# Six graph heads to a turn and to a value product, label sums and key counts in one set of products, first transfers in a fixed order

## What is computed

```python
# layer 0 (shift, scale and gates come from silu(cond) @ w_ada)
k, q, v = split(modulate(ln(x)) @ w_qkv)
x = x + gate_msa * (softmax(q k / 8) v @ w_proj + b_proj)
x = x + gate_mlp * (gelu(modulate(ln(x)) @ w_mlp1 + b_mlp1) @ w_mlp2 + b_mlp2)
# layer 1
self_feat = concat(x, q) @ W_self.T + b_self
for d in range(2):
    A = (adj if d == 0 else swapaxes(adj, 1, 2))[:, :, :20, :]
    aff = where(A.sum(-1) > 0, qh kh / sqrt(8), -9e15) + A @ w_bias + b_bias
    out += softmax(aff) @ self_feat[:, :20] @ Wout[d] + bout[d]     # per head
return x + relu(self_feat + out)
```

## Time and profile before

| | us |
|---|---|
| median of 3 runs (lowest, highest) | 95.21 (93.9, 97.48) |
| the profiled execution: its time | 95.97 |
| its span, first to last instruction | 94.2 |
| around the span | 1.77 |
| busy: PE, DVE, ACT, POOL | 82.9, 69.2, 58.0, 55.7 |

### The profile page before, as it was taken

How to read it: one execution, slowest core, us unless ns; L and a number is a source line. 1 busy time by engine, 2 the same in 40 slices (tenths; PEclk the granted TensorE clock), 3 DMA queues, 4 the chain that set the end, 5 groups by cost and what they waited for, 6 DMA issues and landing times.

```text
span 94.2 us, 4503 instructions
## 1 busy us (share of the span) xinstructions
PE 82.9 (88%) x1936; PEld 64.6 (69%) x1936; DVE 69.2 (73%) x201; ACT 58.0 (62%) x118; POOL 55.7 (59%) x80
## 2 busy tenths in 40 slices
PE   5979999897879999999999977999999989695930
PEld 5968867474657667879767865888777775485810
DVE  3789999898888623577397794598934986779881
ACT  2928629256766559399835888799962496251710
POOL 6769998998952322614463465698407508916640
PEclk9999999999999999999999999999999999999999
DMA  1867754587702370000110000002100021003134
GB/s 36 214 203 241 248 121 156 123 274 206 266 6 55 104 140 7 0 0 7 39 39 7 0 0 10 0 0 46 39 7 0 7 62 27 7 0 74 33 94 114
DMA packets 5971, 7.09 MB, mean 75 GB/s; under 512 B 1024, under 2 KB 4768, under 8 KB 5952
## 3 DMA queue, kind: packets, MB, share of 16 engines
q1 hardware_dynamic: 5664, 6.68, 25.8%
q10 hardware_dynamic: 288, 0.13, 0.5%
HBM read 4.94 MB, written 0.54 MB: 58 GB/s over the span
## 4 chain that ended last, share of the span: by engine, by line
PE 54%; DVE 16%; issue 12%; SPq 6%; DMA 5%; POOL 4%; POOLq 1%
PE ps_all L1063 7%; PE ps_all L1142 6%; PE ps_all L1155 6%; PE ps_all L1106 5%; DMA Vz<-v_raw 5%; PE ps_all L986 4%; SPq L874 4%; PE ps_all L1174 4%; PE ps_all L1069 4%; PE ps_all L1091 3%; PE ps_all L1002 3%; PE ps_all L1096 3%; PE ps_all L1077 2%; PE ps_all L1093 2%; SPq L847 2%
## 5 line engine op out<-in xcount | busy, mean ns | idle before, releaser
L1290 ACT ACTIVATE PT<-ps_all 128x512 f32<-128x512 f32 x24 | 14.1, 596 | 12.9 <-PE ps_all L1155 12.8
L1155 PE MATMUL ps_all<-ident,E 128*128 128x128 f32 x96 | 14.5, 278 | 1.0 <-DVE E L730 1.0
L1155 PEld LDWEIGHTS ps_all<-ident,E 128*128 128x128 f32 x96 | 10.8, 140 | 3.1 <-issue 1.5
L1470 DVE TENSOR_TENSOR E<-ps_all,bias_dir 128x320 f32<-128x320 f32 x16 | 7.8, 489 | 5.2 <-PE ps_all L1142 3.7
L720 POOL TENSOR_TENSOR xT<-gated,xT 128x256 f32<-128x256 f32 x8 | 5.8, 728 | 9.4 <-issue 7.8
L952 POOL TENSOR_TENSOR rstd<-var_eps,minus_half 128x2 f32<-128x2 f32 (+1 forms) x9 | 6.0, 667 | 6.6 <-DVE var_eps L1318 6.3
L1063 PE MATMUL ps_all<-xm,w_rest_sb 128*128 128x256 f32 x32 | 9.7, 390 | 0.0
L730 POOL TENSOR_TENSOR E<-E,neg_max 128x320 f32<-128x320 f32 x8 | 6.2, 774 | 5.4 <-DVE neg_max L1480 5.4
L1223 ACT ACTIVATE hidden<-ps_all,cols 128x256 f32<-128x256 f32 x16 | 7.1, 477 | 3.5 <-PE ps_all L1063 3.4
L1174 PE MATMUL ps_all<-Vz,PT 128*32 128x36 f32 x512 | 7.2, 200 | 1.2 <-issue 1.2
L1174 PEld LDWEIGHTS ps_all<-Vz,PT 128*32 128x32 f32 x512 | 5.9, 109 | 2.7 <-issue 1.4
(11 more groups left out here) (112 smaller groups left out, 201.7 us busy)
## 6 DMA issues: line engine op xcount, KB each, us to landing
home_a<-in_adj SPq DMA_DIRECT2D x2, 448.0 KB, 5.0
Vz<-v_raw SPq DMA_DIRECT2D x16, 45.0 KB
w_rest_sb<-in_w_rest SPq DMA_DIRECT2D x1, 576.0 KB, 5.2
xT<-in_xT SPq DMA_DIRECT2D x1, 512.0 KB
home_a<-in_adj SPq DMA_DIRECT2D x1, 512.0 KB, 4.0
w_rest_sb<-in_w_rest SPq DMA_DIRECT2D x1, 512.0 KB, 5.7
q_tok<-q_rows SPq DMA_DIRECT2D x4, 128.0 KB, 3.5
Vz<-v_raw SPq DMA_DIRECT2D x12, 36.0 KB, 3.1
```

The lines of the kernel that those rows point to most:

```text
L1155: ins = pe.transpose(ps[:, j * P:(j + 1) * P], E[:, r, j * HI:(j + 1) * HI, :], ident[:, :])
L1290: ins = act.activation(PT[:, key % RING, :, :], ps[:, :].rearrange("p (j t) -> p j t", t=P), ACT.Exp)
L1470: ins = dve.tensor_tensor(e_of(key).rearrange("p (j i) k -> p j i k", j=HJ), ps_scores(key), bias_dir[:, d, g, 0:M].unsqueeze(1).unsqueeze ...
```

## The change

- **Turns and values of layer 1.** The arguments of a unit stand as 16 heads of 20 keys without gaps (320 columns and 40 of padding). A turn is three transposes of 120 columns (six heads each), `exp` works on 120 x 384 in place of 128 x 512, and a `values` stage is 3 x 4 products of 54, 54 and 36 columns in place of 4 x 4 of 36.
- **V's places.** `Vz1` has three slots of its own (no part of `Vz0` is reused), each cleared by POOL (2592 columns); mid 3 takes slot 0 again after mid 0's units. A mid's spread is eight DMAs (four of 20 rows with three blocks, four of 20 rows with one) in place of four.
- **Bias.** The adjacency is cut at 121, 121 and 110 rows, 11 whole keys each. One `sel` has label weights in columns 0 to 10 and ones in columns 16 to 26, so that one set of 3 x 4 products without accumulation gives sums and counts. A new DVE stage `btake` (two of them) transposes the results to SBUF; `pen` and `bdir` then read SBUF.
- **Order.** `ORDER` and `BANKS` are new throughout. ACT issues x's group 0 alone; SP issues the others in the order cols, x1, ada0, qkv, x2, x3, x4, ada1. Of the GELU and exp stages, which need different function tables on ACT, all of layer 0's exp now stand ahead of the first GELU and all GELU ahead of layer 1's first exp.

```diff
-ADJ_ROWS = [(0, 112), (112, 224), (224, 352)]
+SIX = 6
+CH = 3
+KR = SIX * M
+EW = CH * KR
+VSLOTS = 3
+KPC = 11
+ADJ_ROWS = [(0, 121), (121, 242), (242, 352)]
...
+BIAS_PARTS = [(0, 1), (2,)]
...
- ('fetch', 'x1'): 'act',
+ ('fetch', 'x1'): 'sp',
...
-        Vz1 = sb("Vz1", [P, HI, (B - VZ0_MIDS_END) * DIRS, HJ, CW])
+        Vz1 = sb("Vz1", [P, VSLOTS, SIX, CH, UB12, DIRS, CW])
...
-        E1 = sb("E1", [P, RING, H, S])
+        E1 = sb("E1", [P, RING, EW])
...
         def vz1_free(m):
-            if batches("v1", m)[2].stop <= VZ0_MIDS_END:
-                return [("values", n) for n in L0_UNITS]
-            return [("zero", ("vz1", m))]
+            if v_before(m) is None:
+                return [("zero", ("vz1", m))]
+            return [("values", n) for n in units_of_mid(v_before(m))]
...
-                    for i in range(HI):
-                        q = slice(QUAD * i, QUAD * i + M)
-                        sp.dma_start(Vz[q, i, :, :, :], v1_raw[q, bs, :, :, :].rearrange("p b d j w -> p (b d) j w"))\
-                          .then_inc(spread_done[key], 16)
+                    nb, k = bs.stop - bs.start, vslot_of(m)
+                    for i in range(SIX):
+                        to = slice(M * i, M * i + M)
+                        for c in range(1 if i < HI else 2):
+                            quad, j, c1 = (i, 0, CH) if i < HI else ((i - HI) * 2 + c, CH, c + 1)
+                            of = slice(QUAD * quad, QUAD * quad + M)
+                            sp.dma_start(Vz1[to, k, i, c:c1, 0:nb, :, :].rearrange("p c b d w -> p c (b d w)"),
+                                         v1_raw[of, j:j + c1 - c, bs, :, :].rearrange("p c b d w -> p c (b d w)"))\
+                              .then_inc(spread_done[key], 16)
...
-                            ins = pe.matmul(ps[QUAD * b:QUAD * b + QUAD, which * G * S:(which + 1) * G * S],
-                                            sel[0:n, which, c, :], t, start=(c == 0), stop=(c == 2))
+                            ins = pe.matmul(ps[QUAD * b:QUAD * b + QUAD, i * G * S:(i + 1) * G * S], sel[0:n, :], t,
+                                            start=True, stop=True)
...
-                    E = E1 if layer_of(key) else E0
-                    for j in range(HJ):
-                        ins = pe.transpose(ps[:, j * P:(j + 1) * P], E[:, r, j * HI:(j + 1) * HI, :], ident[:, :])
+                        for c in range(CH):
+                            ins = pe.transpose(ps[0:KR, c * P:(c + 1) * P], E1[:, r, c * KR:(c + 1) * KR], ident[:, :])
...
-                        for j in range(HJ):
+                        for c in range(CH):
+                            heads = min(SIX, H - c * SIX)
+                            n, w = heads * M, heads * CW
                             for b in range(UB):
...
+                                V = Vz1[0:n, vslot_of(m), 0:heads, c, (g - MIDS[m][0]) * UB + b, d, :]
+                                ins = pe.matmul(ps[QUAD * b:QUAD * b + QUAD, o + c * SIX * CW:o + c * SIX * CW + w],
+                                                PT[0:n, key % RING, c, b * S:(b + 1) * S], V, start=True, stop=True)
...
+                elif stage == "btake":
+                    for s in fresh("dve", ("dense", ("bias", key)), ("adjf", 1)):
+                        dve.wait_ge(*s)
+                    part = BIAS_PARTS[key]
+                    ins = dve.transpose(sums[:, :, part[0]:part[-1] + 1, :].rearrange("p g c k -> p c g k"),
+                                        psum_of(("bias", key))[:, 0:len(part) * G * S]
+                                        .rearrange("p (c g q) -> p c g q", g=G, q=S))
...
-                    ins = dve.tensor_scalar(pen[:, :], psum_of(("bias", 0))[:, G * S:2 * G * S], 0.0, NEG, ALU.is_le,
+                    ins = dve.tensor_scalar(blocks(pen), blocks(sums)[:, :, S // 2:S // 2 + KPC], 0.0, NEG, ALU.is_le,
                                             ALU.mult)
```

More of the change, by code:

```diff
@@ L180 @@
  ('scores', 2): 4,
- ('turn', 2): 3,
- ('values', 2): 3,
+ ('turn', 2): 1,
+ ('values', 2): 2,
  ('scores', 3): 4,
- ('turn', 3): 0,
+ ('turn', 3): 2,
  ('scores', 4): 4,
  ('turn', 4): 0,
- ('values', 3): 3,
+ ('values', 3): 0,
  ('scores', 5): 4,
- ('turn', 5): 0,
+ ('turn', 5): 3,
  ('scores', 6): 4,
- ('turn', 6): 3,
- ('values', 4): 0,
+ ('turn', 6): 1,
+ ('values', 4): 2,
  ('scores', 7): 4,
[L194 to L199, removed]
@@ L200 @@
- ('mlp1', 0, 0): 2,
+ ('turn', 7): 2,
+ ('bias', 0): 3,
+ ('bias', 1): 3,
+ ('yT', 0): 1,
+ ('proj', 0): 0,
+ ('x1tok', 0): 1,
+ ('xn2T', 0): 4,
+ ('mlp1', 0, 0): 1,
  ('mlp1', 0, 1): 6,
- ('mlp1', 0, 2): 0,
- ('mlp1', 0, 3): 1,
+ ('mlp1', 0, 2): 5,
+ ('mlp1', 0, 3): 6,
  ('mlp2', 0): 6,
[L205 to L223, removed]
+ ('self', 0): 5,
+ ('selfT', 0): 5,
+ ('x2tok', 0): 2,
+ ('k1', 0, 0): 2,
+ ('q1', 0, 0): 0,
+ ('k1', 0, 1): 7,
+ ('q1', 0, 1): 2,
+ ('v1', 0, 0): 6,
+ ('v1', 0, 1): 3,
+ ('scores', 8): 4,
+ ('turn', 8): 1,
+ ('values', 5): 6,
+ ('scores', 9): 4,
+ ('turn', 9): 2,
+ ('scores', 10): 4,
+ ('turn', 10): 3,
+ ('values', 6): 3,
+ ('scores', 11): 4,
+ ('turn', 11): 3,
@@ L224 @@
  ('yT', 1): 2,
- ('proj', 1): 1,
+ ('proj', 1): 2,
  ('x1tok', 1): 4,
- ('xn2T', 1): 4,
- ('mlp1', 1, 0): 3,
+ ('xn2T', 1): 2,
+ ('mlp1', 1, 0): 2,
  ('mlp1', 1, 1): 2,
[L230 to L251, removed]
+ ('mlp1', 1, 2): 6,
+ ('mlp1', 1, 3): 7,
+ ('mlp2', 1): 2,
+ ('self', 1): 1,
+ ('selfT', 1): 1,
+ ('x2tok', 1): 1,
+ ('k1', 1, 0): 3,
+ ('q1', 1, 0): 3,
+ ('k1', 1, 1): 0,
+ ('q1', 1, 1): 2,
+ ('v1', 1, 0): 1,
+ ('v1', 1, 1): 2,
+ ('scores', 12): 4,
+ ('turn', 12): 4,
+ ('values', 7): 7,
+ ('scores', 13): 4,
+ ('turn', 13): 7,
+ ('scores', 14): 4,
+ ('turn', 14): 5,
+ ('values', 8): 0,
+ ('scores', 15): 4,
@@ L252 @@
+ ('turn', 15): 7,
  ('yT', 2): 5,
[L253 to L256, removed]
+ ('proj', 2): 3,
+ ('x1tok', 2): 4,
+ ('xn2T', 2): 4,
+ ('mlp1', 2, 0): 7,
  ('mlp1', 2, 1): 5,
- ('mlp1', 2, 2): 6,
+ ('mlp1', 2, 2): 3,
  ('mlp1', 2, 3): 6,
[L260 to L269, removed]
+ ('mlp2', 2): 3,
+ ('self', 2): 0,
+ ('selfT', 2): 0,
@@ L284 @@
- ('mlp1', 3, 0): 4,
+ ('xn2T', 3): 0,
+ ('mlp1', 3, 0): 3,
  ('mlp1', 3, 1): 0,
- ('mlp1', 3, 2): 2,
- ('mlp1', 3, 3): 7,
- ('mlp2', 3): 5,
+ ('mlp1', 3, 2): 1,
+ ('mlp1', 3, 3): 1,
+ ('mlp2', 3): 0,
  ('self', 3): 4,
  ('selfT', 3): 4,
[L291 to L296, removed]
+ ('x2tok', 3): 6,
+ ('k1', 3, 0): 6,
+ ('q1', 3, 0): 4,
+ ('k1', 3, 1): 5,
+ ('q1', 3, 1): 4,
+ ('v1', 3, 0): 6,
  ('v1', 3, 1): 0,
  ('scores', 20): 4,
- ('turn', 20): 3,
@@ L515, in freed_by @@
     if kind == "bias":
[L516 removed]
+        return [("btake", user[1])]
     if kind == "warm":
```

385 lines of the change are left out of this document (200 added, 185 removed), and 3 rows, old and new, of the table ORDER.

## The result

The changed kernel takes 91.81 us in the median of four runs, the kernel before 95.81 in the same runs: a ratio of 0.9655, 95% interval 0.9553 to 0.9756, so 3.5% faster (2.4 to 4.5%), 3.3 us; the medians differ by 4.0. The prediction was 91.5 us. Profiled execution against profiled execution it is 91.11 against 95.97 us (spans 89.4 and 94.2), 4.9 us, where the prediction had 3.7; that pair makes the gain too large.

What follows compares the result with a forecast made beforehand. DVE bounds layer 0's attention, PE the MLPs and bias, neither the graph attention. Savings of 1.4 + 1.1 + 0.8 + 0.4 = 3.7 us take 95.97 to 92.3 us, or 91.5 against the median; range 89.2 to 95.6.

Steps and rivals of the forecast that it cites:

- Bias products, -1.4: Graph bias products on PE: one set in place of two, whole in the chain, saves 1.4 us; bounds -1.4 and 0.
- Turns, -1.1: Layer 1's turns: three transposes in place of four save a quarter of the chain's pieces, 1.1 us; bounds -2.1 and 0.
- values, -0.8: Layer 1's value products: fewer products per unit, time going by count rather than columns, saves 0.8 us; bounds -1.7 and 0.
- Start, -0.4: First modulation weights: issued earlier behind one transfer, shortening PE's 0.49 us wait, saves 0.4 us; bounds -0.5 and 0.
- ACT's loads, 0: Fewer function table loads take 5.1 us from ACT, outside the chain, so counted at nothing; bounds -2 and 0.
- Sixteen more DMAs: Layer 1's spreads: the last mid's longer issue and landing, up to 7.1 us, tie with other work: 0; bounds 0 and +2.4.
- POOL's clears, 0: Clearing three larger slots, 2.27 us each, adds 2.8 us on POOL, counted at nothing; bounds 0 and +2.3.
- rival 2: POOL holds DVE: one clear between statistics and the next MLP loses 2.3 us of the gain; 93.8 us, chance 0.08.
- ORDER, a shift that costs nothing if the rest is denser: Graph attention starts later, first `badd` about 50.3 us; costs nothing if DVE is then 82% busy, against 77% before.
- rival 1: Graph attention gets no denser: DVE stays at 77%, the gain is 1.1 us; 94.1 us, chance 0.22.
- rival 3: Slower: graph attention's late start isn't made good, DVE 70% busy, ending 3.1 us later; 98.3 us, chance 0.14.
- rival 4: PE's waits swallow the shorter stages, as the chain goes elsewhere; 95.2 us, chance 0.04.

Runs made afterwards that it cites:

- put-back run: The changed kernel with only the fourth transpose of a turn and the 8 more value records of a unit put back: 93.38 us, 0.9843 of the kernel before.
- base run: The changed kernel itself, unaltered, timed again beside the follow-up kernels: 92.15 us, 0.9655 of the kernel before.
- the run with two queues: The changed kernel with three mid 3 instructions moved, and three of its last spread's eight DMAs issued on ScalarE's queue: 93.0 us, 0.987 of the kernel before.

## Why the prediction came out right, and where its steps did not

**Bias products, -1.4.** 24 records in some 1.4 us, as said. The worth was about half: 0.6 to 0.7 us, with intervals of 2% either way. The step that failed is "they stand where PE has no idle time": true of the old order's profile, but in the new one the first two thirds stand early, ahead of a wait that they shorten.

**Turns, -1.1, and values, -0.8.** 1.2 to 1.8 us together by the put-back run, 1.9 predicted. A turn of three transposes is 0.33 us, and the 48 records of a pair's values take 0.73 us, 15 ns each (0.66 and 14 at the best). So the count decides more than the columns: 13.4 ns by the earlier trace rows, 18 by columns.

**Start, -0.4.** The wait of 0.49 us in the earlier trace rows is gone, as said. Undoing it in the new order costs 1.6 us by the ratios: more than the term, since in the profile of that run a little more idle time there was followed by a fall of the granted clock. The change need not have gained 1.6 from it against the kernel before, whose mean granted clock was 1.00 in its profile.

**ACT's loads, 0.** Not contradicted for the old order, to about 1 us. For the new order the run with four more shows that it has no room for them where they were put.

**Sixteen more DMAs, "a tie", taken at 0.** This was mis-sized. I took 0.6 us a DMA from layer 0's; those of layer 1 take more, 0.71 us in the median of the sixteen in the kernel before and 0.77 of the 32 in the base run. The chain of the base run, from the last transpose of V:

```profile
74.95 0.81 SPq L898
...
75.81 0.79 SPq L898
...
80.59 1.83 DMA Vz<-v_raw
```

The eighth issue starts at 80.59 and ends at 81.30, which makes 6.35 us for the eight, against 4.8; the last piece runs from that start to the landing at 82.42, 1.1 us behind the issue. From V to the landing it is 7.5 us, against "up to 7.1". PE waited 0.59 us in that run, 0.86 in the other. The prediction named such a wait as a sign that it is wrong; it cost less than the gains elsewhere, so as a sign against the whole forecast it was too strong.

**POOL's clears, 0, and rival 2.** Three clears take 2.26 us each and none is in the chain; `rstd`'s groups are near 0.7 us. The mechanism of rival 2 did strike, at another place: not a clear and `pen`, but the product of the keys of mid 3 beside a subtraction, 1.1 us. The Trainium skill, SBUF — State Buffer, section "Who interferes with whom", says that a DVE instruction with two SBUF inputs conflicts with a GpSimd one that reads SBUF and that the one issued second waits out the first; the two rows at 70.07 us agree, and 0.48 us with the two apart agrees too.

**ORDER, a shift that costs nothing if the rest is denser.** The first `badd` came at 49.75 us (50.3 predicted), 31.98 us of DVE were left (31.6), and DVE was busy 87% (82 needed, 77 for rival 1, 70 for rival 3). This is the step on which the forecast rested, and it held. But the density isn't the order's alone: with turns and values as long as before the new order has 82%, and the old order with short stages 79%. So the sum, which counted stages whole and the order at nothing, had the two apart where the profiles show them to depend on each other. Rivals 1 and 3 fell with the density, and rival 4 ("PE's waits swallow the shorter stages") with the time; in the old order it describes what part of the gain met.

The sum is right in total and partly by luck. Its 3.3 us for the three stages is what they cost when all are put back (3.1 by the ratios), though one by one they cost 0.7 and 1.8. All the rest, the start and what was counted at nothing, came to 0.2 us of gain (0.9983) where the sum had 0.4, with an interval of 3% either way. In that rest the spread's wait and the stalled subtraction (0.9 and 1.1 us) were left out, so something else must have given about as much. That it is idle time of PE which the new order removed is likely by the tables above, but how it divides among loads, layer 0's spreads, the start and the rest was not tried.

## What to carry to other kernels

The pieces of the chain tell what a shorter stage is worth only in the order, and strictly in the execution, that they were read in. Before counting a stage's saving whole, look for the wait that it runs into next; where an order is written out by hand, shorten the stages and make the order anew together, and time each alone, with executions enough, to see which of the two carries it. For DMAs that are issued one by one, take the issue time from the very transfer's line, not from a similar one.

## What the runs showed of the hardware

- After 0.3 us of delay at the start and some more idle time up to 9 us, the granted clock was 0.50 (the 1.2 GHz level) from 9 to about 18 us in one profile (the run with the old first transfers); mid 0's `mlp2` came 4.1 us later there than in the changed kernel.
- A DMA of 20 partitions of the spread held its issuing queue for 0.71 to 1.09 us on SP (median 0.77 of 32, three blocks or one, base run) and for 0.72 to 1.33 on ACT (three of one block, the run with two queues); ACT started no other instruction from 76.57 to 79.41 us, while it issued them.
- Table loads of 1.283 us cost nearly their whole time ahead of takes that PE reads (4.7 of 5.1 us for four, give or take 2.2). Six in the old order, 7.7 us, cost nothing that the runs can tell (1.1 us less by the medians, 1.2 more by the ratio). ACT's next instruction started 0.01 us behind a load (57.54 + 1.28, then 58.83, in the changed kernel).
- A DVE subtraction of SBUF tiles took 1.58 us when it started 0.01 us behind a POOL product of SBUF tiles of 1.25 us, and 0.48 us where that product came 1.7 us later.
